# A graph network's node tiles, ring places and arrival counts, packed several to a 32-bit word

## What is computed

```python
def spmm(h):
    msg = h[src] * edge_w[:, None]
    agg = segment_sum(msg, dst, N)
    return agg + self_w[:, None] * h
h = spmm(x @ W1 + b1)
h = relu((h - bn_mean) * rsqrt(bn_var + eps) * bn_gamma + bn_beta)
x = layernorm(x + spmm(h @ W2 + b2))

q, k, v = x @ q_w.T + q_b, x @ k_w.T + k_b, x @ v_w.T + v_b      # (n, 8, 16)
scores = einsum('ehd,ehd->eh', q[src], k[dst]) / sqrt(16) + edge_attr @ eb_w.T + eb_b
attn = exp(scores - segment_max(scores, src)[src]); attn /= segment_sum(attn, src)[src] + 1e-10
out = segment_sum(attn[..., None] * v[dst], src, n)
x = layernorm(x + out @ out_w.T + out_b)
```

## Time and profile before

| | |
|---|---|
| median of 3 runs | 9242.84 us (9242.41 to 9247.89) |
| the profiled execution's own time | 9239.79 us |
| its span | 9238.2 us |
| granted TensorE clock, mean | 0.792 |
| busy: PE, PE's weight loads, DVE | 6786.1 (73%), 5668.8 (61%), 5985.6 us (65%) |
| busy: ACT, POOL | 3366.2 (36%), 5983.4 us (65%) |

### The profile page before, as it was taken

How to read it: one execution, slowest core, us unless ns; L and a number is a source line. 1 busy time by engine, 2 the same in 40 slices (tenths; PEclk the granted TensorE clock), 3 DMA queues, 4 the chain that set the end, 5 groups by cost and what they waited for, 6 DMA issues and landing times. The chain is left out here.

```text
span 9238.2 us, 229276 instructions
## 1 busy us (share of the span) xinstructions
PE 6786.1 (73%) x40334; PEld 5668.8 (61%) x40335; DVE 5985.6 (65%) x23214; ACT 3366.2 (36%) x11074; POOL 5983.4 (65%) x6648
## 2 busy tenths in 40 slices
PE   7789999999958888888886556666666577736773
PEld 5578888888847777777774344444444466625663
DVE  8855555555547777777776655555555566687777
ACT  7633333333324444444442100000000244417884
POOL 4467777666656666666666577777777555526664
PEclk9876666666668888888886787887888899978997
DMA  1044333333342211111112333333333555515553
GB/s 46 8 112 106 105 102 104 101 103 102 92 123 53 53 51 51 51 50 50 49 49 58 102 112 113 113 112 112 112 112 112 143 138 138 138 50 139 150 154 90
DMA packets 1057789, 868.52 MB, mean 94 GB/s; under 512 B 214824, under 2 KB 950424, under 8 KB 1057736
## 3 DMA queue, kind: packets, MB, share of 16 engines
q0 software_dynamic: 179664, 437.87, 15.7%
q1 hardware_dynamic: 643032, 319.49, 13.1%
q10 hardware_dynamic: 235040, 110.58, 4.2%
HBM read 578.04 MB, written 287.84 MB: 94 GB/s over the span
## 5 line engine op out<-in xcount | busy, mean ns | idle before, releaser
L1420 POOL DMA_INDIRECT spmm_rows<-h_table,spmm_index_ring x3136 | 2972.3, 948 | 1469.3 <-issue 883.1
L1491 PE MATMUL bank<-spmm_rows,spmm_hot 128*128 x6660 | 1951.4, 395 | 119.7 <-SPq L1397 78.0
L1765 POOL DMA_INDIRECT kv_sorted<-expand_payload,expand_where_ring x1568 | 1521.3, 970 | 501.1 <-issue 418.9
L1465 DVE TENSOR_TENSOR region_ab<-region_ab,bank 128x128 f32 x3330 | 953.0, 286 | 1216.1 <-PE bank L1491 1171.2
L1786 PE MATMUL bank<-region_ab,expand_hot_t 128*128 x3336 | 1109.4, 490 | 771.4 <-DVE expand_hot_t L1802 770.3
L1491 PEld LDWEIGHTS bank<-spmm_rows,spmm_hot 128*128 128x128 f32 x6660 | 1420.7, 265 | 216.8 <-issue 187.1
L1818 DVE SCALAR_TENSOR_TENSOR expand_payload<-expand_payload,region_c,bank 128x256 f32 x1668 | 801.0, 480 | 896.8 <-SPq L1730 412.8
L1786 PEld LDWEIGHTS bank<-region_ab,expand_hot_t 128*128 128x128 f32 x3336 | 766.5, 241 | 977.1 <-issue 849.5
L1449 DVE TENSOR_SCALAR spmm_hot<-iota_bf,lo_slots 128x128 f32<-128x128 bf16 x3334 | 999.0, 300 | 20.0 <-issue 18.7
L456 ACT ACTIVATE spmm_beside_sign<-iota_half,region_c 128x128 bf16<-128x128 bf16 x1568 | 521.8, 392 | 827.9 <-DVE spmm_beside_bias_sb L545 678.9
L689 PE MATMUL bank<-spmm_beside_next_slot,spmm_beside_lo_t 128*128 128x98 f32 x3136 | 808.5, 346 | 0.4
(11 more groups left out here) (350 smaller groups left out, 13765.0 us busy)
## 6 DMA issues: line engine op xcount, KB each, us to landing
score_k_rows<-kv_sorted SPq DMA_DIRECT2D x420, 288.0 KB
mix_mixed<-kv_sorted SPq DMA_DIRECT2D x420, 256.0 KB
spmm_beside_attr_sb<-in_edge_attr_dram ACTq DMA_DIRECT2D x390, 256.0 KB
spmm_rows<-h_table,spmm_index_ring POOLq DMA_INDIRECT x3136
kv_sorted<-expand_payload,expand_where_ring POOLq DMA_INDIRECT x1568
kv_sorted<-spmm_beside_blank SPq DMA_DIRECT2D x1, 15232.0 KB
kv_sorted<-spmm_beside_blank SPq DMA_DIRECT2D x98, 136.0 KB
h_table<-region_ab SPq DMA_DIRECT2D x28, 448.0 KB, 3.0
```

The lines of the kernel that those rows point to most:

```text
L1420: nc.gpsimd.indirect_dma_start(rows[:, h * HALF + k, :], None, table, bass.IndirectOffsetOnAxis(ap=index_ring[:, h, k:k + 1], axis=0)).the ...
L1465: nc.vector.tensor_tensor(here, here, sum_bank[k % 2][:, 0:D], ALU.add).then_inc(added, 1)
L1491: nc.tensor.matmul(sum_bank[k % 2][:, 0:D], hot[:, k % HOTS, :], tile_of(rows, place[k % HALF]), start=True, stop=True).then_inc(summed, 1)
L1765: nc.gpsimd.indirect_dma_start(kv_sorted, bass.IndirectOffsetOnAxis(ap=where_ring[:, h, k:k + 1], axis=0), payload[:, h * HALF + k, 0:ROW] ...
```

## The change

A new tile `words` holds the same numbers packed: four node tiles or places to a 32-bit word as bytes, two counts to a word as 16-bit halves. `node_words` are the node tiles by destination, `turn_words` those of the score loop, `sum_words` the places of mix. `half_words` holds four words for each half of 8 tiles: two with the eight ring places and two with four counts. Only every second tile's count is kept, the later one's, and PE and DVE wait for `arrived` and `freed` once per pair of tiles. Each engine loads the packed words and cuts a number out by shift and mask (`byte_of`, `half_of`); the lowest byte of a word needs the mask alone. Four copies (three in `window_slots`, one in the score stage) fill the words from the rows; the rows of mix are written packed at once. `place_i` in `window_slots` now lies over another tile.

```diff
+        HALF_WORDS_LOADED = 4
+        words = sb("words", [PLACE_ROW + 1, S_TILES // HALF * HALF_WORDS_LOADED], I32)
+        half_words = words[0:1, :]
+        node_words, turn_words, sum_words = (words[row:row + 1, 0:S_TILES // 4] for row in (S_ROW, UNTIL_ROW, PLACE_ROW))
...
+        def byte_of(words, k, top):
+            return ((words[k // 4] >> (8 * (k % 4))) & 255).with_bounds(min_val=0, max_val=top)
+        def half_of(words, k, top):
+            return ((words[k // 2] >> (16 * (k % 2))) & 65535).with_bounds(min_val=1, max_val=top)
...
# window_slots, DVE
-                    place_i = tmp("place_i", [P, S_TILES], I32)
+                    place_i = passed.bitcast(I32)
...
+                    link(v.tensor_copy(node_words.bitcast(U8), node_d))
+                    link(v.tensor_copy(half_words.bitcast(U8).rearrange(...)[:, :, 0:HALF], in_halves(window_place)))
+                    link(v.tensor_copy(half_words.bitcast(I16).rearrange(...)[:, :, HALF // 2:],
+                                       in_halves(until_window)[:, :, 1::2]))
                     dve.wait_ge(keys_in, 16 * W_BLOCKS)
...
# sparse_product, DVE
-                            node = loaded(mybir.EngineType.DVE, node_d[0:1, bass.ds(i * TURN + h * HALF, HALF)], HALF, NT - 1, CLAMPED)
+                            node = loaded(mybir.EngineType.DVE, node_words[:, bass.ds((i * 2 + h) * (HALF // 4), HALF // 4)], HALF // 4, MOST, PACKED)
...
                                 dve.wait_ge(summed, t + 1)
                                 need(dve, added, t)
-                                here = tile_of(nodes, node[k % HALF])
+                                here = tile_of(nodes, byte_of(node, k % HALF, NT - 1))
...
# sparse_product, PE
-                                place = loaded(mybir.EngineType.PE, window_place[:, some], HALF, TURN, WINDOW_SLOT)
-                                until = loaded(mybir.EngineType.PE, until_window[:, some], HALF, E_COLS, CLAMPED, least=1)
+                                half = loaded(mybir.EngineType.PE, half_words[:, bass.ds(..., HALF_WORDS_LOADED)],
+                                              HALF_WORDS_LOADED, MOST, PACKED)
...
-                            pe.wait_ge(arrived, until[k % HALF])
-                            nc.tensor.matmul(sum_bank[k % 2][:, 0:D], hot[:, k % HOTS, :], tile_of(rows, place[k % HALF]),
+                            if k % 2 == 0:
+                                pe.wait_ge(arrived, half_of(half, HALF // 2 + k % HALF // 2, E_COLS))
+                            nc.tensor.matmul(sum_bank[k % 2][:, 0:D], hot[:, k % HOTS, :], tile_of(rows, byte_of(half, k % HALF, TURN)),
...
# expand, PE: one word per group
-                        node = loaded(mybir.EngineType.PE, node_d[0:1, bass.ds(i * TURN + j * GROUP, GROUP)], GROUP, NT - 1, CLAMPED)
+                        node = loaded(mybir.EngineType.PE, node_words[:, bass.ds(i * GROUPS + j, 1)], 1, MOST, PACKED)
...
# expand, DVE: four words per two groups
-                        place = loaded(mybir.EngineType.DVE, window_place[:, some], GROUP, TURN, WINDOW_SLOT)
-                        until = loaded(mybir.EngineType.DVE, until_window[:, some], GROUP, E_COLS, CLAMPED, least=1)
+                        if j % 2 == 0:
+                            half[:] = loaded(mybir.EngineType.DVE, half_words[:, bass.ds(..., HALF_WORDS_LOADED)],
+                                             HALF_WORDS_LOADED, MOST, PACKED)
...
-                            dve.wait_ge(freed, until[m])
+                            if m % 2 == 0:
+                                dve.wait_ge(freed, half_of(half, HALF // 2 + j % 2 * (GROUP // 2) + m // 2, E_COLS))
...
# score, PE: four words per turn
-                        node = loaded(mybir.EngineType.PE, node_at[0:1, bass.ds(i * TURN + j * GROUP, GROUP)], GROUP, NT - 1, CLAMPED)
+                        if j == 0:
+                            node[:] = loaded(mybir.EngineType.PE, turn_words[:, bass.ds(i * GROUPS, GROUPS)], GROUPS, MOST, PACKED)
...
-                                                    tile_of(nodes, node[n]), start=True, stop=True)
+                                                    tile_of(nodes, byte_of(node, j * GROUP + n, NT - 1)), start=True, stop=True)
...
# score, DVE
+                v.tensor_copy(turn_words.bitcast(U8), node_at).then_inc(nodes_placed, 1)
...
# mix, DVE: four words per turn
-                    _, place = nc.values_load_multi_w_load_instructions(
-                        sum_places[:, bass.ds(i * TURN, TURN)], engines=[mybir.EngineType.DVE],
-                        min_val=0, max_val=NT, skip_runtime_bounds_check_because=CLAMPED)
+                    place = loaded(mybir.EngineType.DVE, sum_words[:, bass.ds(i * GROUPS, GROUPS)], GROUPS, MOST, PACKED)
...
-                                here = tile_of(sums, place[k * 2 + stream])
+                                here = tile_of(sums, byte_of(place, k * 2 + stream, NT))
```

23 lines of the change are left out of this document (15 added, 8 removed).

## The result

The change is slower: 9891.5 us against 9243.2, a ratio of 1.070 (95% interval 1.068 to 1.072), so 7% or some 648 us (medians of four runs each). The profiled execution has a span of 9884.3 us at a mean granted clock of 0.763 (before: 9238.2 at 0.792).

A forecast was written before the change was run, and what follows sets the result against it. No engine bounds throughout: POOL's scatters set expand, PE and DVE the second product, PE's sequencer score, DVE's mix. Terms 30 - 50 + 0 + 107 + 145 = +232 us on 9239.8 gave 9472, range 9225 to 9690.

The forecast's parts named there:

- Expand, 0: Expand stage: POOL's 1.275 us per scatter covers PE's and DVE's loads and operations; 0, without that cover some 60 us.
- Score, +107: Score stage: per turn three loads saved at 0.5 us, 28 operations added at 0.09 on PE's sequencer; +107 us.
- Mix, +145: Mix stage: DVE's load 0.76 us shorter per turn, 28 operations lengthen the chain of adds by 2.52; +145 us.
- DVE's load, -0.38 us: Sparse products: DVE's load per half, shortened from 8 words to 2, was to save 0.38 us.
- The first product, +30: First sparse product: PE's array covers its sequencer, one 0.17 us charged per half for DVE; +30 us (0 to +50).
- covers the sequencer: First product: PE's array, busy 1905 of 2120 us, was to hide the 20 added operations per half.
- The second product, -50: Second sparse product: PE's load gap shrinks by 1.0 us per half, part gained; -50 us, bounds -200 and +157.
- a quarter of the gain: Second product: as DVE is near its own end, only this share of PE's smaller gap counts; -50 us.
- 0.17 us per tile between sum and add: Sparse products: delay by DVE's operations behind the wait for the sum; charged once per half in the first, 196 x 0.17.
- the second, both sequencers as the bound: Much slower: 20 operations make PE's sequencer the bound in both products, +314 us, 9806 in all; chance 0.10.
- The first rival: Faster by the clock: shorter gaps keep the second product's clock up, -300 us there, 9070 in all; chance 0.12.
- the bounds of score and mix: Limits of these two stages' terms: score -63 to +233 us, mix 0 to +273 us.

The follow-up runs named there:

- g3: Changed kernel, both engines' product operations ahead of the waits; score two plain 8-word loads, mix late plain load: products 2143 and 2363 us.
- h3: Changed kernel with PE's product loads plain, DVE packed with bytes ahead of the sum's wait, plain score and mix: products 2013 and 2229 us, total 9135.
- e3: Changed kernel with plain words in the products but a wait per pair, score's bytes ahead of its waits, mix as changed: score 1025, mix 823 us.
- e4: Changed kernel with product operations ahead of the waits and two operations more per tile in score and mix: score 1368, mix 1070 us.

## Why the prediction was wrong

The direction and the stages of score and mix were right; the size was not: +232 us forecast, 9472, against 9891, outside the range.

- **Expand, 0**: right, -2 us. POOL's scatters set it.
- **Score, +107**: measured +139, within the bounds. The mechanism was right, PE's sequencer pays. The operation was mis-sized: 0.097 to 0.10 us in place of 0.09. The prediction also held against this term the page "TensorE: Matmul & The Clock Gate" of the Trainium skill, section "Architectural detail: the array is 16× 32×32, not 1× 128×128", with its queue of 64 entries. Taken so that such a queue hides the operations, it does not agree with this stage, where each added one cost 0.10 us and nothing of it was hidden.
- **Mix, +145**: measured +113. The place in the chain was right; an operation costs 0.074 there, not 0.09. The 0.76 us of shorter load came back (138.4 - 60.5 = 78 us). That score and mix together came out at the +252 that was forecast is luck: one was 32 us too low, the other 32 too high.
- **DVE's load, -0.38 us**: 2 words took 529 ns where 0.22 us was extrapolated; it saved 0.07.
- **The first product, +30** is the first step that failed, in the sentence that PE's array "covers the sequencer". PE's packing alone cost 79 us, though the array was busy 91% of the loop before, and the two engines together 165.
- **The second product, -50** is the second step that failed, and the larger. PE's gap did shrink by 1.0 us a half, but "a quarter of the gain" let through was wrong in sign. With PE's part alone changed, 153 us of waiting for DVE's one-hots took the place of the 198 us of gap, so little of the gap came back: the wait that ended next was DVE's. PE's busy time, with the operations between its matmuls, grew by 100 us (1931.86 against 1831.25), and the product became 76 us longer. Second, the prediction named 0.17 us per tile between sum and add (by its own price it is 14 x 0.09 / 8 = 0.16), and charged it once per half in the first product and not at all in the second. It comes with every tile, and in the second product PE waits for one-hots that stand behind that add: 144 us for DVE's side, measured alone, or 0.09 per tile, and 3 when the same operations are moved ahead of the wait.
- **The rivals**: the second, both sequencers as the bound, had 0.10 and 9806 us, the nearest number. Its mechanism was half right: PE's operations do cost in both products, at 0.03 each and not 0.09, and the rest was DVE's place and the two together. The first rival wanted the clock of the second product to rise over 0.9; it fell, from 0.83 to 0.79 over the edge loop.
- **The range** ended at 9690, which was said to hold the bounds of score and mix together with half of the second rival's price. By the prediction's own figures these are 9240 + 233 + 273 + 157 = 9903, so its own sum reached past the measured time.
- **The clock as a cause.** Both products lost clock (0.63 to 0.58, 0.83 to 0.79), and this was a rival to every sequencer's price. From the window matmuls that start at either level I estimate that 20 to 45 of the 165 us and 30 to 50 of the 237 go with the longer time at the lower level; the rest is there at each level by itself.

What stays open: whether the wait per pair is part of PE's +76 in the second product; why both engines' packing together cost 69 us more in the first product than the sum of each alone; and why PE's packing with both engines' operations ahead of the waits (g3) cost 130 and 134 us over h3, more than with DVE plain.

## What to carry to other kernels

Price a register operation by the distance from its start to the next one's, not by its duration (here 97 ns on PE and 74 on DVE, for durations of 32 to 45), and then by where it stands. Ahead of a wait that the engine would stand at anyway, it was free (h3); ahead of the wait in mix, where DVE sets the pace, 0.04 us of it showed. Between a wait and the instruction that others wait for, it cost 0.05 (second product) to 0.07 us (mix), and on PE's sequencer, where that sets the pace, 0.10. Fewer words to load is worth little beside moving the load to where the engine is computing, as the plain late load of mix showed, or cutting one long stop into two. And where two engines hand work to each other tile by tile, a shorter stop on one may only show the next wait, so the edit on each engine is to be tried alone.

## What the runs showed of the hardware that was not expected

- A register load's time doesn't follow its words: 1 word took 301 ns on PE (expand, changed kernel), 2 words 529 on DVE, 4 words 332 to 346, 8 words 589 to 601, 16 words 1107. A strided load of 4 words took 993.
- Register operations in a row start 97 ns apart on PE's sequencer and 74 ns on DVE's (e3, e4, changed kernel), two to three times their duration, and on PE at any granted clock alike.
- In score one 16-word load on PE per turn went with a granted clock of 0.92, two loads of 8 words with 1.00 (2.4 GHz all through), and the stage was 45 us shorter, with the same work, some 30 of them (my estimate) at the full clock as well. With the change's operations the clock was 0.92, with about twice as many 0.58.
- DVE's sequencer runs on under DVE's own work when nothing in front of it waits: a plain 16-word load of 1.1 us, put behind a one-hot operation of 0.76 us, gave back 55 of the 123 us that it had cost in front.
